# A fused attention and mixture-of-experts layer on one core: another order of two groups of matmuls on TensorE

## What is computed

```
xn = layernorm(x)
# attention branch: one small table per batch, looked up by index
off = (xn @ W_off + b_off)[..., 0];  w = softmax(xn @ W_attn + b_attn)
idx = clip(where(int(off) < 0, int(off) + 128, int(off)), 0, 127)     # 32 per token
s   = sum(xn[:, 0, :][idx] * w)                                       # one number per token
attn = broadcast(s) @ W_out + b_out
# feed-forward branch, for all 8192 tokens
ffn(x, w1, w2, w3) = (silu(x @ w1.T) * (x @ w3.T)) @ w2.T
shared = ffn(xn, shared 0) + ffn(xn, shared 1)
top 2 of 8 experts by router logits; routed = sum_k weight_k * ffn(xn, expert_k)
out = x + attn + shared + routed
```

## Time and profile before

| | |
|---|---|
| median of 3 runs | 414.48 us (413.73 to 414.81) |
| profiled execution, its own time | 413.19 us |
| its span, from the first to the last instruction | 411.4 us |
| around the span | 1.8 us |
| granted TensorE clock, mean over the span | 0.98 |
| TensorE busy | 367.3 us |
| VectorE busy | 320.9 us |
| GpSimd busy | 226.0 us |

### The profile page before, as it was taken

How to read it: one execution, slowest core, us unless ns; L and a number is a source line. 1 busy time by engine, 2 the same in 40 slices (tenths; PEclk the granted TensorE clock), 3 DMA queues, 4 the chain that set the end, 5 groups by cost and what they waited for, 6 DMA issues and landing times.

```text
span 411.4 us, 12486 instructions
## 1 busy us (share of the span) xinstructions
PE 367.3 (89%) x4333; PEld 316.5 (77%) x4333; DVE 320.9 (78%) x865; ACT 188.9 (46%) x446; POOL 226.0 (55%) x184
## 2 busy tenths in 40 slices
PE   0167798789999999999999999999999999999992
PEld 0055575467677777777779999999999999999992
DVE  5988989987987799999996768766666666666662
ACT  2778729295432466776666444322222222222220
POOL 0434500402877777343300999548876667766776
PEclk9977999899999999999999999999999999999998
DMA  8944530000116499977895455786754655543233
GB/s 290 306 103 104 118 90 0 2 0 16 42 50 132 95 165 176 193 167 157 162 130 94 123 178 163 159 105 69 76 61 57 61 74 57 61 56 35 27 33 33
DMA packets 98870, 41.35 MB, mean 101 GB/s; under 512 B 73600, under 2 KB 92416, under 8 KB 98816
## 3 DMA queue, kind: packets, MB, share of 16 engines
q1 hardware_dynamic: 87120, 31.82, 38.5%
q0 software_dynamic: 11264, 8.69, 15.7%
q10 hardware_dynamic: 432, 0.11, 0.2%
HBM read 10.94 MB, written 12.88 MB: 58 GB/s over the span
## 4 chain that ended last, share of the span: by engine, by line
PE 77%; DVE 12%; ACT 5%; DMA 2%; issue 2%; POOL 1%; POOLq 0%; DVEq 0%; ACTq 0%
PE pY L833 18%; PE pY L666 12%; PE pAB L807 8%; PE pAB L809 8%; PE pAB L808 8%; PE pAB L654 5%; PE pAB L656 5%; PE pAB L655 5%; PE pV L678 4%; ACT units L886 2%; PE pV L624 2%; ACT wsp L957 2%; DVE hbuf L1223 2%; DVE hot L1129 1%; DMA xT<-hot 1%
## 5 line engine op out<-in xcount | busy, mean ns | idle before, releaser
L1081 POOL DMA_INDIRECT out_dram<-xT,rows x64 | 99.2, 1550 | 47.1 <-DVE xT L1574 23.0
L1069 POOL DMA_INDIRECT sorted_rows<-rows,slot x64 | 67.2, 1050 | 59.1 <-issue 33.3
L1030 ACT ACTIVATE units<-pAB 128x512 f32<-128x512 f32 x78 | 46.4, 594 | 109.9 <-PE pAB L809 109.1
L807 PE MATMUL pAB<-rows,wsp 128*128 128x128 f16 x512 | 87.6, 219 | 0.0
L808 PE MATMUL pAB<-rows,wsp 128*128 128x128 f16 x512 | 87.6, 219 | 0.0
L809 PE MATMUL pAB<-rows,wsp 128*128 128x128 f16 x512 | 87.6, 219 | 0.0
L1512 DVE SCALAR_TENSOR_TENSOR hbuf<-pAB,units 128x512 f32<-128x512 f32 x78 | 53.5, 687 | 37.3 <-PE pAB L809 36.5
L833 PE MATMUL pY<-wsp,hbuf 128*128 (+1 forms) x620 | 78.9, 279 | 0.4 <-issue 0.4
L833 PEld LDWEIGHTS pY<-wsp,hbuf 128*128 128x128 f32 x620 | 72.7, 192 | 0.9 <-issue 0.9
L666 PE MATMUL pY<-wsp,hbuf 128*128 128x128 f32 x512 | 70.4, 281 | 0.0
L666 PEld LDWEIGHTS pY<-wsp,hbuf 128*128 128x128 f32 x512 | 64.5, 192 | 4.2
(11 more groups left out here) (165 smaller groups left out, 619.3 us busy)
## 6 DMA issues: line engine op xcount, KB each, us to landing
base<-in_x SPq DMA_DIRECT2D x8, 512.0 KB, 7.3
out_dram<-base SPq DMA_DIRECT2D x16, 256.0 KB, 2.5
wraw<-in_wall SPq DMA_DIRECT2D x10, 256.0 KB, 3.0
rows<-hot SPq DMA_DIRECT2D x8, 256.0 KB, 2.7
proj<-sorted_rows SPq DMA_DIRECT2D x27, 68.5 KB, 2.3
wsp<-in_wall SPq DMA_DIRECT2D x10, 128.0 KB
sorted_rows<-rows,slot POOLq DMA_INDIRECT x64, 2.4
out_dram<-xT,rows POOLq DMA_INDIRECT x64, 3.3
```

The costliest lines, as they stand in the source:

```text
L807: pe.matmul(o, hi, x(0), start=True, stop=False)
L1069: pool.indirect_dma_start(sorted_rows, bass.IndirectOffsetOnAxis(ap=slot[:, t:t + 1].bitcast(U32), axis=0), rows[:, t, :], None, bounds_ch ...
L1081: pool.indirect_dma_start(out_rows, bass.IndirectOffsetOnAxis(ap=meta[:, t, DEST - CW:DEST - CW + 1].bitcast(U32), axis=0), yt[:, t], None ...
```

## The change

In the third stage the pick of a unit now stands ahead of its first products instead of behind them. In the last jobs the second products of job 75 (`NJOB - 3`) now stand ahead of the first products of job 77, and VectorE makes the sums of job 75 right behind those of job 74, ahead of the multiplication of job 77.

```diff
-            both = shared[:1] + [(2, pick, ROUND * ATT, UNITS)] + shared[1:]
+            both = [(2, pick, ROUND * ATT, UNITS)] + shared
...
-            for q in range(SINGLE, NJOB + 2):
-                if q < NJOB:
-                    one(r_first, q)
+            for q in range(SINGLE, NJOB - 1):
+                one(r_first, q)
                 one(r_second, q - 2)
+            one(r_second, NJOB - 3)
+            one(r_first, NJOB - 1)
+            one(r_second, NJOB - 2)
+            one(r_second, NJOB - 1)
...
-                for job in (q,) if q >= SINGLE - 2 else (q - 1, q) if q % 2 else ():
+                if q == NJOB - 3:
+                    return
+                for job in (q, q + 1) if q == NJOB - 4 else (q,) if q >= SINGLE - 2 else (q - 1, q) if q % 2 else ():
                     for part in (side_sums, y_first, y_second):
```

## The result

| | before | after |
|---|---|---|
| median | 414.56 us (413.73 to 414.81, 4 runs) | 417.53 us (417.12 to 418.07, 4 runs) |
| ratio, 95% interval | | 1.0078 [1.0057, 1.0099] |
| profiled execution | 413.19 us | 418.07 us |
| its span | 411.4 us | 416.3 us |
| TensorE busy | 367.3 us | 367.6 us |

The changed kernel is slower by 3.0 us. The forecast was 414.2 us with a range up to 415.3, so it was wrong. So I read places and mechanisms from the traces, and sizes from both the traces and the medians.

What follows compares the result with a forecast made beforehand. TensorE was taken to bound the kernel, with VectorE and DMA nearly level in the third stage; gains of 0.1 (stage) + 0.2 (last jobs) = 0.3 us off 414.48 gave 414.2 us, range 412.7 to 415.3.

Steps and rivals of the forecast that it cites:

- TensorE's own saving: Third stage, units 34 to 63: second products always follow first products, saving 30 x 0.081 = 2.43 us of TensorE time.
- Pick and then F costs nothing: Third stage: first products right behind a pick pay 0 for their weight load, against a bound of 0.08 us.
- Rival B: Third stage: the pick's neighbour pays 0.08 us ahead of each unit's first products; 414.9 us, chance 0.08.
- The limit by `weigh`: Third stage: picks wait for VectorE's weigh two picks back, capping the 2.43 us saving at about 1.1 us.
- The transposes: Third stage: pick 26 waits for its transpose, leaving 0.4 us; pick 10's wait, through VectorE, leaves 0.1 us.
- They come no earlier: Third stage: SP issues transposes when VectorE has written a batch, so the change does not make them earlier; no separate size.
- a price through VectorE: Third stage: pick 10's late transpose idles VectorE before multiplication 46 by about 0.3 us, passed on to pick 26.
- C: Third stage: transposes 10 and 26 land later than shown, delays going through in full; 415.2 us, chance 0.09.
- From 223 us on TensorE is the chain without a break, so what the stage gives is kept: After the third stage, 223 to 404 us: TensorE alone is the chain, so the stage's gain is kept in full.
- The last jobs: Tail: gain 0 if the end hangs on job 74's send, 0.4 us if that delay is accidental; 0.2 taken.
- A: Third stage: transposes are not late, so only the weigh limit counts; gain 1.5 us, 413.0 us, chance 0.24.
- D: Whole change: everything is worth it if VectorE too gets quicker, up to 2.4 + 0.4; 411.7 us, chance 0.04.

Runs made afterwards that it cites:

- picks behind S: Kernel before, with each pick moved behind its unit's second products and the last jobs unchanged: 413.87 us, ratio 0.9983.
- the loop cut: Changed kernel, with VectorE writing a unit's quarter of the one-hot rows ahead of its multiplication: 414.82 us, ratio to before 0.9997.
- before with the dose: Kernel before, with one 4-byte DMA issued by SP in front of the first transpose of batches 1 to 7: 414.61 us, ratio 1.0011.
- both attempts: Kernel with picks behind S, plus first main rows issued ahead of transpose 28: 413.30 us; or plus two small loads on GpSimd's queue: 413.55 us.

## Why the prediction was wrong

**TensorE's own saving: right.** S takes 0.88 to 0.89 us in the units of the stage, a unit without a wait 2.65, and 30 x 0.081 us are saved.

**Pick and then F costs nothing: right.** F starts 0.47 us behind the start of a pick that did not wait. The load time that the Trainium skill, "TensorE: Matmul & The Clock Gate", section on LDWEIGHTS, gives (columns / 1.2 ns, 107 ns for 128 columns) is near the 98 ns of the earlier trace rows. The estimate that was worked out from it, 78 ns of load standing bare in front of F, does not agree with this trace: the figure is the length of a load, and the load is hidden here. Rival B is out.

**The limit by `weigh`: right in kind.** With the picks behind S the stage keeps VectorE's pace of 10.83 us for four units from pick 16 on, and with the loop cut two picks wait for `weigh`. In the changed kernel it never comes to that.

**The transposes: the step that failed.** The prediction's term for them was a wait of P(10) and one of P(26), counted once each, which left 0.1 us of gain in the stage. Measured are six waits of the first picks, 5.6 us with what follows them, and a stage that ends 3.1 us later. The prediction looked at transposes 10 and 26 because their landings were recorded, and took them for the slowest. How late a pick is depends on issue and need together, and the first pick of a batch has the least in hand: its transpose is issued last relative to it. The trace of before would have allowed the sum. Transpose 8 was issued at 156.46 there, and the quickest landing of the earlier trace rows is 3.8 us, 160.3. Pick 8 was at 161.71 and wanted at 161.71 - 1.29 - 8 x 0.081 = 159.8. So it was late by 0.5 us even with that one. In the two traces with the old order of picks that record it (the last jobs alone, and before with the dose) transpose 8 took 4.2 us, which makes it 0.9. The transposes named did land as forecast, 5.4 us (10) and 6.0 us (26) behind their issue, and neither pick waited, as the first pick of the batch had waited already.

**"They come no earlier": true, and taken for the whole.** What was left out is that they can come later. The one-hot rows need nothing of TensorE as data, but on VectorE's stream they stand behind a multiplication that does. So a late pick makes the next batch late. The prediction counted such a wait once with a price through VectorE (0.3 us). It comes back each lap: 11.5 us for a lap of the loop on the mean, against 10.6 that TensorE wants, where the order of before had 1.5 us in hand by the estimate above. The rival that came closest was C, by late transposes through VectorE; its price was 0.9 and its chance 0.09, since it was tied to transposes 10 and 26 landing later than shown, which in the trace of after they did only by 0.1 us (26) or not at all (10). No rival's time reached the 417.53 us measured.

**"From 223 us on TensorE is the chain without a break, so what the stage gives is kept": wrong in both directions.** The turn of the second extra job waits for the end of SP's row of issues; without the two small loads in that row the wait is gone and 1.4 us of the changed kernel's loss with it. So a delay of SP costs there, and a gain of TensorE is taken back there (1.2 of 1.95 us with the picks behind S). That a shorter row then gives this gain back is not shown: both attempts fell short of it. The chain of before showed TensorE and could not show who stood 0.1 us behind it.

**The last jobs: the order costs nothing, as worked out, and of the two values for the gain 0 is the right one.** The wait ahead of job 74's send stands in every trace (1.36 to 1.41 us), so the 0.2 that I took between 0 and 0.4 was 0.2 too much. It is small beside the rest.

**Rivals A and D: out.** Both needed transposes that don't make TensorE wait.

**What stays open.** In the profiled executions the loss is 4.9 us, by the medians 3.0. The stage's 3.1, 1.35 more at the turn (4.45 in all) and 0.3 up to the last send make up nearly all of the former; the kernel before may meet part of the turn's wait in other executions than the one profiled (0.4 us in the kernel with only the last jobs changed), but the small loads moved there gave nothing, which speaks against much of it.

## What to carry to other kernels

Before an instruction that waits is moved ahead of others, follow what it holds up in a circle: through each engine's stream, not only through the data, back to what it waits for, and compare that circle's length with the pace of the busiest engine. Look for the item with the least between its arrival and its use (here the first of each batch), not for the slowest transfer, nor for those whose landing happens to be recorded. Where a stage's gain is to be kept, ask what is second at each wait behind it: here one row of issues on SyncE, which two small loads on another queue shortened by enough.

## What the runs showed of the hardware

- A first transpose of a batch landed 3.2 to 5.1 us behind its issue over all traces, the later ones up to 6.5 us; the issue alone holds SP for 1.23 us and up to 3.59 (picks behind S).
- Loads of 128 columns in fp16 (98 ns) follow 29 ns apart inside a pick, and the following F starts as close behind; S in fp32 right behind a pick pays 0.08 us. F behind a pick that had waited starts 0.1 us later (0.57 in place of 0.47 us behind the pick's start).
- With TensorE idle for 1.74 us between 225 and 228 us, the granted clock was 0.52 from 228 to 231, and the way to the next turn was 1.36 us longer (one execution). With 1.24 us of idle time in the same stretch (picks behind S, all loads on SyncE) it was 1.00.
- A DMA of 4 bytes costs SP 0.29 us of its row, and a load at an address from a register 0.83 us (224.56 - 223.73).
